# Four consecutive tokens per partition in the rows read back from the experts, and four filler products instead of eleven

## The reference, cut to what matters

```python
h = layernorm(x) * (1 + ca) + sa
x = x + ga * attention(h)
h = layernorm(x) * (1 + cb) + sb
x = x + gb * experts(h)
```

```python
idx = argmax(h @ router)
y   = (silu(h @ gate[idx]) * (h @ up[idx])) @ down[idx]     # block 1: times 2 * the chosen probability
ys  = (silu(h @ gate_s) * (h @ up_s)) @ down_s
experts(h) = y + ys
```

## Time and profile before

| what | value |
|---|---|
| median of 3 runs | 1019.22 us |
| lowest and highest of them | 1019.07 and 1022.32 us |
| the profiled execution, its own time | 1016.15 us |
| its span, from the first to the last instruction | 1014.4 us |
| mean granted clock of PE, as a share of 2.4 GHz | 0.991 |
| busy share of PE, DVE, ACT, POOL | 92%, 62%, 55%, 45% |
| HBM read, written | 31.32 MB, 18.69 MB |

### The profile page before, as it was taken

The page is one execution under the profiler, slowest core; times in us unless marked ns, Lnnn a source line. Parts: engine busy times, 40 slices in busy tenths (PEclk is TensorE's granted clock), DMA queues, the critical chain, the costliest instruction groups (busy, mean ns, idle before and its releaser), DMA issues.

```text
span 1014.4 us, 21471 instructions
## 1 busy us (share of the span) xinstructions
PE 937.2 (92%) x7349; PEld 595.8 (59%) x7349; DVE 624.7 (62%) x2060; ACT 553.4 (55%) x1077; POOL 461.5 (45%) x697
## 2 busy tenths in 40 slices
PE   8999999999989979999889988889997899999997
PEld 4566777777754223334433886456664544499994
DVE  4788888888815976863733544567874563344444
ACT  5536676667667554565511555547775622245551
POOL 1146777776742946620074454335453044323331
PEclk9999999999999999999999999989999999999999
DMA  6720000000011000040012224200000000121115
GB/s 212 245 72 13 9 11 13 13 7 13 13 52 42 0 0 1 0 166 0 1 54 61 61 77 145 62 2 1 2 2 1 1 29 30 32 62 50 49 30 176
DMA packets 38617, 45.95 MB, mean 45 GB/s; under 512 B 7872, under 2 KB 31936, under 8 KB 37648
## 3 DMA queue, kind: packets, MB, share of 16 engines
q1 hardware_dynamic: 34000, 35.26, 11.3%
q0 software_dynamic: 4512, 9.32, 2.8%
HBM read 31.32 MB, written 18.69 MB: 49 GB/s over the span
## 4 chain that ended last, share of the span: by engine, by line
PE 80%; ACT 7%; DVE 6%; issue 4%; POOL 1%; DMA 1%; another core or an unknown queue 1%; DVEq 0%; SPq 0%; ACTq 0%; POOLq 0%
PE PS L696 6%; PE PS L451 5%; PE PS L493 5%; PE PS L679 4%; PE PS L686 4%; PE PS L347 4%; PE PS L639 4%; PE PS L632 4%; PE PS L464 4%; PE PS L630 4%; PE PS L356 3%; PE PS L553 2%; PE PS L380 2%; PE PS L789 2%; PE PS L444 2%
## 5 line engine op out<-in xcount | busy, mean ns | idle before, releaser
L917 ACT ACTIVATE pw<-PS 128x384 f32<-128x384 f32 x256 | 111.5, 488 | 71.3 <-PE PS L473 68.6
L1604 POOL TENSOR_SCALAR_AFFINE_SELECT pw<-pw 128x256 f32<-128x256 f32 x256 | 105.1, 434 | 74.8 <-ACT pw L917 72.9
L1199 DVE CUSTOM_DVE_ANT_0 PS<-PS,above 128x256 f32<-128x256 f32 x256 | 115.7, 452 | 31.4 <-PE PS L444 31.2
L1670 POOL DMA_INDIRECT token_rows<-xnb,slot_in x77 | 73.9, 959 | 118.3 <-ACT xnb L1027 110.9
L1656 POOL TENSOR_TENSOR XS<-XS,N 128x512 f32<-128x512 f32 x64 | 81.2, 1292 | 54.4 <-DVE N L1277 33.7
L451 PE MATMUL PS<-kf,qm 32*128 32x256 f32 x512 | 103.3, 426 | 0.5 <-POOL qm L1613 0.5
L1456 DVE TENSOR_TENSOR rsb<-sqb,PS 128x256 f32<-128x256 f32 (+1 forms) x77 | 42.6, 553 | 92.3 <-PE PS L686 54.8
L1201 DVE CUSTOM_DVE_ANT_0 PS<-PS,above 128x128 f32<-128x128 f32 x256 | 84.5, 330 | 0.0
L1626 POOL TENSOR_SCALAR_AFFINE_SELECT pw<-pw 128x256 f32<-128x256 f32 x128 | 56.1, 472 | 62.1 <-ACT pw L1072 62.1
L1010 ACT ACTIVATE sqb<-PS 128x512 f32<-128x512 f32 x48 | 28.7, 597 | 96.5 <-PE PS L630 77.9
L1613 POOL TENSOR_SCALAR qm<-qs,qmask 128x256 f32<-128x256 f32 x64 | 59.7, 934 | 45.2 <-ACT kf L898 45.2
(11 more groups left out here) (214 smaller groups left out, 2358.2 us busy)
## 6 DMA issues: line engine op xcount, KB each, us to landing
sorted_rows<-empty_rows_dram SPq DMA_DIRECT2D x2, 2535.0 KB, 14.4
slot_in<-sorted_rows SPq DMA_DIRECT2D x77, 65.0 KB
N<-token_rows SPq DMA_DIRECT2D x16, 256.0 KB, 4.8
X<-xT_dram SPq DMA_DIRECT2D x8, 256.0 KB, 5.8
token_rows<-empty_rows_dram SPq DMA_DIRECT2D x1, 2048.0 KB, 23.9
ATT<-gate_dram SPq DMA_DIRECT2D x1, 2048.0 KB
XS<-down_dram SPq DMA_DIRECT2D x1, 2048.0 KB
H<-up_dram SPq DMA_DIRECT2D x1, 2048.0 KB
```

The costliest lines, as they stand in the source:

```text
L917: nc.scalar.activation(pw[:, w % 2, j + n, :], PS[:, A_PST + (2 * v + n) % 3, 0:3 * P], ACT.Exp).then_inc(a_p, 1)
L1199: nc.vector.tensor_tensor_reduce(x[:, 0:SEQ], x[:, 0:SEQ], above[:, :], 1.0, -3e38, ALU.add, ALU.max, mx[:, t // 8 % 2, 1, j, g:g + 1])
L1604: m = nc.gpsimd.affine_select(x[:, :, SEQ * k:SEQ * k + P], x[:, :, SEQ * k:SEQ * k + P], [[0, 2], [1, P]], ALU.is_ge, 0.0, base=0, channe ...
L1670: nc.gpsimd.indirect_dma_start(token_rows[l][:, :], bass.IndirectOffsetOnAxis(slot_in[:, r, D:D + 1].bitcast(mybir.dt.int32), 0), slot_out ...
```

## The change

Three edits. The rows of a chunk are read back so that partition p receives the tokens 4p to 4p + 3 of the chunk, one after the other (2048 bytes that are contiguous in DRAM and in the partition), instead of the tokens p, p + 128, p + 256 and p + 384 (four pieces of 512 bytes). A tile that PE turns then holds every fourth token, so the transposed columns are written to PSUM with a step of four elements (16 bytes) instead of next to each other, and the bank ends up in the same order as before. In block 0 four filler products run instead of eleven.

```diff
@@ returned, on SP
                     sp.dma_start(N[:, n * CH:(n + 1) * CH].rearrange("p (n d) -> p n d", d=D),
-                                 token_rows[l][n * CH:(n + 1) * CH, :].rearrange("(n p) d -> p n d", p=P)
+                                 token_rows[l][n * CH:(n + 1) * CH, :].rearrange("(p n) d -> p n d", p=P)
                                  ).then_inc(chunk_in[n], 16)
@@ moe, on PE
                 if l == 0:
-                    idle(11, 5)
+                    idle(4, 5)
@@ turn_back, on PE
+                by_row = PS[:, 6 + k % 2, :].rearrange("d (p n) -> d n p", n=4)
                 for n in range(4):
-                    m = nc.tensor.transpose(PS[:, 6 + k % 2, n * P:(n + 1) * P], N[:, k * CH + n * P:k * CH + (n + 1) * P],
-                                            ident[:, :])
+                    m = nc.tensor.transpose(by_row[:, n, :], N[:, k * CH + n * P:k * CH + (n + 1) * P], ident[:, :])
                 m.then_inc(q["back"], 1)
```

## The result

The changed kernel takes 1014.11 us (median of 11 runs, 1009.62 to 1016.3). The kernel before, run beside it on the same chip, takes 1019.95 us (11 runs, 1019.07 to 1023.64). The ratio is 0.9936 [0.9919, 0.9953], a gain of 6.5 us in 1020 with an interval from 4.8 to 8.3; the two medians differ by 5.8. The forecast was 5.6 us and 1013.6 us, so the number came out right. On two other chips, where all the experiments ran, most of this gain is missing. Why it is there on one chip and not on the others is the larger part of what follows.

The account below looks back on a forecast made before the run. PE was taken as the bound, busy 92% of the span and 80% of the chain. Fillers 4.5 plus reads 1.1, step 0, gave 5.6 us off a median of 1019.22: 1013.6 us, range 1010.5 to 1019.0.

Parts of the forecast that it names:

- Seven fillers fewer: Before slot loop 0 in block 0: four fillers instead of eleven start the loop 4.5 us earlier, at 554.48 instead of 559.00.
- The bound of 6.0: Before slot loop 0: upper end of the fillers' gain, 6.0 us, if the slots landed by the fourth filler's end.
- The clock falls in the new gap: Rival, chance 0.14: PE's wait before slot loop 0 lowers the clock, costing at most 1.7 us, 1015.3 us in all.
- Reads in pieces of 2048 bytes: Read-back of block 0: larger pieces save 0.2 us a chunk and bring the first centring product 1.1 us earlier.
- The chain's wait for `N`: Read-back of block 0: PE's waiting for the reads of `N`, 4.93 us before, would come near 4 us.
- The limit by DVE: Read-back of block 0: DVE's additions, 0.87 us a chunk, let the turn of chunk 4 start at 637.0 at the earliest.
- its own later limit, 637.2: Read-back of block 0: the time at which the read lets the turn of chunk 4 start, against 637.0 by DVE.
- The rival that the reads are no faster: Rival, chance 0.07: reads in the read-back gain nothing, so only the fillers' 4.5 us remain, 1014.7 us.
- The step in PSUM: Turns of the read-backs: writing columns with a step of four costs 0, bounded above by 1.28 us a chunk.
- The two rivals built on a cost: Turns in both read-backs: step costs 0.64 us a chunk (1018.7 us, chance 0.18) or 1.28 (1028.2 us, chance 0.09).
- The end of the program: Last read-back, block 1: DVE's additions and PE's turns alternate without DMA in the chain, so faster reads gain 0.
- The sum: Whole kernel: 4.5 + 1.1 = 5.6 us gained, a median of 1013.6 us; forecast's chance 0.52.

Follow-up runs that it names:

- the probe: The changed kernel with its four fillers replaced by four groups of four 512-column products, fp32 and bf16, each in order and with a step of four: 998.63 us.

## Why the prediction was right, and where it was not

**Seven fillers fewer, 4.5 us: right on the chip it was made for, by one profile each.** SP's read to gate product went from 7.39 to 2.80 us, 4.6 won, and the read's own time of 1.99 us, borrowed from block 1, came out as 1.92. The bound of 6.0 was reached in the profiled execution, counted from the first filler. Not all of it was kept: slot loop 0 behind it is 0.9 us longer, where I had written that the loop moves along. But one premise was silent: that PE comes to the fillers 3 us ahead of SP's read. That was a row of one execution. It is 1.6 us in the profile of the change, and 6.0 us in each profile on the other chips, where the same seven fillers bring 1.4 us at the start. Two things set the distance, POOL's row of scatters and the standstill of ACT and DVE that holds PE up ahead of the fillers, and I costed neither. I wrote that the first slot read is late next; I should have asked what releases that read, and how far it can move against PE.

**The clock falls in the new gap, chance 0.14, cost at most 1.7 us: wrong for the other chips.** With four fillers there, PE waited 4.1 to 4.2 us and the clock fell to 0.50 in all four profiles; with none, a wait of 8.87 us, it fell to 0.50 as well; with eight, waits of 0.8 to 0.95 us, it stayed at 1.00 in four profiles of four. The price in the loop was 0.8 to 2.4 us. The term of 1.7 us came from a single fall of 3.4 us, and with the new reads and four fillers the clock was low for 6.8 us, twice as long. On the first chip PE's weight load waited 0.61 us and the clock stayed at 1.00 from 552 to 558, as forecast.

**Reads in pieces of 2048 bytes, 1.1 us: right in kind, too large.** The rate rose from 308 to 379 GB/s. I had taken 406 from the read of `X`, its best microsecond. The turn of chunk 4 came 0.4 us sooner behind SP's first read, the first centring product 0.5 us sooner in the table and no sooner in the profile of the result. The failed term is five chunks times 0.2 us. With 379 GB/s a chunk saves 262144 / 308 - 262144 / 379 = 0.16 us, and five of these would be 0.8. The larger miss is that not every chunk saves it: chunk 2 follows chunk 1 by 1.15 us before and 1.43 now, chunk 3 follows by 1.29 and 1.19, both longer than the 0.69 us that a chunk takes at 379 GB/s, and what holds them up is not shown. The chain's wait for `N`, forecast near 4 us, went from 4.93 only to 4.81. The limit by DVE that I named is there too: with the new reads and eleven fillers it is DVE's addition that releases the turn of chunk 4, and no longer the read. The sum had a slip besides, for by its own later limit, 637.2, the part is 1.0 and not 1.1. In whole times the part is 0.998 [0.9964, 0.9996] with eleven fillers and nothing to be told with eight (0.9965 against 0.9968). The rival that the reads are no faster is wrong by the trace; that they are worth less than the spread of runs is closer.

**The step in PSUM, taken as 0: right.** The turns are 273 ns with it and without. The reason I gave was that a turn leaves the write more time, and the probe fits it by its rates: four turns follow each other 0.11 to 0.12 us apart, about 0.9 ns for each of their 128 columns, where the probe's bf16 products take 0.42 ns a column in order and 0.84 with the step. The 0.42 ns are also what the prediction's 0.053 us for 128 columns come to. That a turn goes through twice was my reading of 0.11 against 0.053 us; measured is the ratio of two. The two rivals built on a cost (0.64 and 1.28 us a chunk) are out.

**The end of the program, 0: right.** The chain has the same two terms.

**The sum.** 4.6 + 0.4 = 5.0 us by the stretches of the two profiles, or 6.4 if the start is counted from the first filler; measured are 6.5 [4.8, 8.3]. That this fits so well is in part luck. In the same two profiles the slot loop takes 0.9 us of it back and the fall of the clock at 635 the 0.4, so 3.7 us are left from SP's first slot read to the first centring product, and 2.4 in the spans. One profile of each kernel can't tell more, and no run on that chip divides the 6.5 us into parts.

On the other chips the three right columns of the table add up to 79.5 us for the kernel before, 79.5 to 80.1 with four fillers and 76.7 to 77.6 with eight. That accounts for the lead of eight over four (2.5 and 3.1 us by the table, 2.1 and 2.0 measured), and for 1.9 to 2.8 of the 3.2 to 3.8 us that eight fillers bring against the kernel before. The rest stays open.

## What to carry to other kernels

Work that is there to keep PE's clock up has a right amount: here the best that ran ended 0.8 to 0.95 us before the data landed, and the clock stayed at 1.00. With four the wait left was 4 us, the clock fell to 0.50, and that took back what the earlier start brought (1.4 won, 2.2 lost); with eleven the last 1.7 us were pure delay. The distance between PE's arrival and SP's read differs from chip to chip, and on one of them from run to run (1.6 and 3.0 us on the chip of the result, 6.0 on the others), so a number found on one need not be the best on another: eight beat four by 2 us where they were run, and were not run on the chip of the result.

A gain from removed filler is to be predicted from what releases the next step, followed back to its own engine (here POOL's last scatter), and from what can make PE itself late, and not from the one distance that a single trace shows.

## What the runs showed of the hardware

- The same program takes 1020 us on one chip and 1000 us on two others. Slot loop 0 alone, from the first gate product to SP's read-back, is 71.9 us on the first (630.91 - 559.00) and 61.2 us there: 10.7 of the 20 us. On the first chip PE waits in it 6.2 us for copies of DVE and ACT, in sixteen waits between 559 and 625, on the other 0.6 us in one. Another 6.4 us lie ahead of the fillers, where ACT and DVE stand still on the first chip alone (from POOL's first scatter to the first filler 42.1 us against 35.7).
- The granted clock was at 0.50 for 3.4 us around the first turns with four fillers and the old reads, for some 6.8 us with the new ones, and for 10.2 us without fillers. Such stretches stand at other places too, and not at the same ones in two profiles of one kernel: with eight fillers and the new reads, both profiles have one from about 651 to 658, and only one of them has another from 641.5 to 644.9.
- A step of four elements on a PSUM output doubles the probe's bf16 product of 512 columns (0.43 against 0.215 us) and costs an fp32 product or turn nothing (sixteen records in 7.10 us, eight of them with a step, against 7.11 and 7.10 with none; turns of 273 ns with it and without).
- In block 0's read-back SP issues eight transfers of the same 256 KB in 3.64 us when their pieces are 2048 bytes and in 4.7 to 5.4 us when they are 512 bytes. Most start 0.47 us apart with the large pieces and 0.55 us with the small ones; the eighth small one starts 0.8 to 1.6 us behind the seventh, and the traces don't tell why. The median from issue to landing went from 4.8 to 4.5 us in the two profiles of the first chip.
